# Splitting GpSimd's 128x512 additions and subtractions into two of 128x256

## The chip, the cores and the metric

The kernel runs on one core of one Trainium2 chip. The metric is the device time of one execution in microseconds (us), the median of three. TensorE is PE in the rows, its weight loads are PEld, VectorE is DVE, ScalarE is ACT, GpSimd is POOL, and SyncE with the DMA queue that it feeds is SP.

## The reference

64 sequences of 256 tokens with 256 features go through one decoder block. There are three attentions of 16 heads each, then a mixture of experts:

```
x = x + self_attention(layernorm(x))      # A: int8-quantized linears, causal softmax
x = x + cross_attention(layernorm(x))     # X: 120 context tokens, key mask, softmax with an extra zero
z = layernorm(x); y = z + self_attention(layernorm(z) * g1 + b1)   # F
x = x + y + moe(layernorm(y) * g2 + b2)   # F's end, then top-2 of 8 experts, 256 -> 1024 -> 256
```

All inputs and outputs are float32. Only the element-wise steps around queries, keys and residuals are touched by the change.

## The kernel before, in words

`attention(..., kind)` is called three times, for kinds A, X and F. Each call is one software-pipelined loop over the 64 sequences. In every turn of the loop each engine works through a fixed list of named steps (`SCHEDULE[kind][engine]`), written out by hand, and `LAG` and `SHIFTED` say for each name to which later or earlier sequence it belongs. So a turn holds parts of about nine sequences at once, and the order inside an engine never changes. The engines meet through semaphores only.

The steps that matter here, by their names in the lists:

- `maxima`: PE forms the scores of one head (L686 in F, L676 the last part in A, L681 in X) in one of three PSUM banks, and DVE reduces them to their maxima (L949). `attend`: PE forms the transposed scores (L658 in F), with ACT taking the exponential (L837). `pv0`, `pv1`: PE multiplies probabilities and values (L719 in F).
- `topA`, `topB`: DVE turns eight heads' maxima into two bfloat16 parts (L960 in A only, L962, L963), which PE transposes in `rowsA`, `rowsB` (L786).
- `q`, `k`: PE projects (L772), ACT evacuates and casts (L896, L911), then GpSimd subtracts the cast from the float32 value into `left` (L1119). `q_rest`, `k_rest`: ACT casts `left` to bfloat16 (L853), then GpSimd subtracts again and writes the third part (L1125). SP stores the three parts (L591), and loads them later in another layout (L536, L539).
- `xT`: PE transposes the normalized input, ACT evacuates it (L878 in F) for `q`.
- `fetch` in X: GpSimd adds a bias to the input (L1131), and DVE adds the projected attention of A to that (L990, step `wo`). `refetch`: GpSimd adds a bias to the residual read back (L1141 in X, L1146 in F), DVE adds the projection (L1083). `uapply` in F: DVE normalizes (`hn`, L1043), GpSimd forms `xu` (L1152) and then `h2 = hn * g` (L1156) and `h2 + b` (L1159), with a semaphore between these two.

GpSimd's and ACT's lists in F are, in order:

```
"POOL": ("k_rest q q_rest uapply refetch k")
"ACT": ("attend attend attend evac1 attend rowsB attend attend k_rest xT attend aT q attend attend q_rest "
        "attend attend rowsA attend evac0 h2T attend attend k attend attend")
```

GpSimd's `k` step and ACT's `k_rest` belong to the same sequence, with ACT's coming one turn list later. ACT goes on to `xT` only after `k_rest`, and PE's `q` waits for `xT`.

Of the kernel before, what the change touches and what calls it, by code (L numbers as in the profile page):

```python
# [5 lines left out]
ALU = mybir.AluOpType  # L6
# [21 lines left out]
def need(eng, sem, value):  # L28

    if isinstance(value, int) and value <= 0:  # L30
        return
    eng.wait_ge(sem, value)  # L32


def hold(eng, sem, value, passed):


    need(eng, sem, value)
    if not isinstance(value, int):
        eng.sem_inc(passed, 1)  # L40
# [306 lines left out]
def attention(nc, C, D, io, scratch, kind):  # L347
# [69 lines left out]
    def total(b, counts):  # L417

        if isinstance(b, int):
            return sum(turns(b, n) * c for n, c in counts)  # L420
        return b * sum(c for _, c in counts) + sum(LAG[n] * c for n, c in counts)

    def filling(g, name):

        b = g - LAG[name]
        if isinstance(b, int):
            n = total(b, [(u, 1) for u in UNITS]) + sum(present(b, u) for u in UNITS[:UNITS.index(name)])
            return n % 2, n // 2
        base = sum(LAG[u] for u in UNITS) + UNITS.index(name)
        return base % 2, NU // 2 * b + base // 2  # L430
# [12 lines left out]
    def iterations(eng):  # L443

        for b in range(FIRST, 3):
            yield b, b % 2
        with eng.Fori(0, (B - 8) // 2) as r:
            yield 2 * r + 3, 1
            yield 2 * r + 4, 0
        for b in range(B - 5, LAST + 1):  # L450
            yield b, b % 2

    def exists(g):

        return not isinstance(g, int) or 0 <= g < B

    def steps(b, par, engine):

        for name, i in STEPS[engine]:
            if present(b, name):  # L460
                yield name, i, b + LAG[name], (par + LAG[name]) % 2

    with ExitStack() as ctx:
# [13 lines left out]
        xin, grid = sb("xin", [P, 2, 256]), sb("grid", [P, 2, 256])  # L477
        xw, xT = sb("xw", [P, 2, 256], xdt), [sb(f"xT{i}", [P, 2, 256], xdt) for i in range(2)]
        q_f, k_f, left = sb("q_f", [P, 2, 256]), sb("k_f", [P, 2, 256]), {n: sb("left_" + n, [P, 2, 256]) for n in "qk"}
# [3 lines left out]
        aT, xres, zres = sb("aT", [P, 2, 256]), sb("xres", [P, 2, 256]), sb("zres", [P, 2, 256])  # L483
        based, summed = sb("based", [P, 2, 256]), sb("summed", [P, 2, 256])
# [12 lines left out]
        if kind == "X":  # L497
            yin, yint, yT = sb("yin", [P, 2, 256]), sb("yint", [P, 2, 256], BF16), sb("yT", [P, 2, 256], BF16)
            xb, x1, cin, ctxT = sb("xb", [P, 2, 256]), sb("x1", [P, 2, 256]), sb("cin", [120, 256]), [sb(f"ctxT{i}", [P, 2, 120]) for i in range(2)]
# [3 lines left out]
            y_in, y_ready, ctx_in, mask_in, mask_ready, maskT_ready, xb_ready, x1_out, xres_in, based_ready, mask_zero = (  # L503
                sem(n) for n in ("y_in", "y_ready", "ctx_in", "mask_in", "mask_ready", "maskT_ready", "xb_ready", "x1_out",
                                 "xres_in", "based_ready", "mask_zero"))
        if kind == "F":
            z, hn, h2, h2T = sb("z", [P, 2, 256]), sb("hn", [P, 2, 256]), sb("h2", [P, 2, 256]), sb("h2T", [P, 2, 256])
            xu = sb("xu", [P, 2, 256])
            ustats, umean_var, rstd_set = sb("ustats", [P, 2, 6]), sb("umean_var", [P, 2, 2]), sem("rstd_set")
            z_out, zres_in, xres_in, based_ready, hn_ready, xu_ready, h2_ready, h2_out = (  # L510
                sem(n) for n in ("z_out", "zres_in", "xres_in", "based_ready", "hn_ready", "xu_ready", "h2_ready", "h2_out"))

        with nc.Block() as block:
# [588 lines left out]
            @block.gpsimd  # L1102
            def _(pool):
                if kind == "X":
                    for m in mask:
                        nc.gpsimd.memset(m[:, :, :], 0.0).then_inc(mask_zero, 1)
                    pool.wait_ge(mask_zero, 2)
                for b, par in iterations(pool):
                    for name, i, g, gp in steps(b, par, "POOL"):
                        def drained(g, name):  # L1110
                            if exists(g):
                                bk, us = filling(g, name)
                                need(pool, work_drained[bk], us + 1)

                        if name in ("q", "k"):
                            src, parts, cast, rest, n = (q_f, q_parts, q_cast0, q_rest, 256) if name == "q" else \
                                (k_f, k_parts, k_cast0, k_rest, KT)
                            pool.wait_ge(cast, g + 1)
                            nc.gpsimd.tensor_tensor(left[name[0]][:, :, 0:n], src[:, :, 0:n], parts[:, 0, :, 0:n], ALU.subtract)\  # L1119
                                .then_inc(rest, 1)  # L1120
                        if name in ("q_rest", "k_rest"):
                            parts, cast, split, n = (q_parts, q_cast1, q_split, 256) if name[0] == "q" else \
                                (k_parts, k_cast1, k_split, KT)
                            pool.wait_ge(cast, g + 1)
                            nc.gpsimd.tensor_tensor(parts[:, 2, :, 0:n], left[name[0]][:, :, 0:n], parts[:, 1, :, 0:n], ALU.subtract)\  # L1125
                                .then_inc(split, 1)
                            pool.wait_ge(split, g + 1)
                        if name == "fetch" and kind == "X":
                            pool.wait_ge(x_in, 16 * g + 16)
                            drained(g - 1, "wo")  # L1130
                            nc.gpsimd.tensor_tensor(xb[:, :, :], xin[:, :, :], C["bo_a"][:, :, :], ALU.add).then_inc(xb_ready, 1)  # L1131
                        if name == "mload":
                            hold(pool, mask_in, 16 * g + 16, C["passed"])
                            hold(pool, score_full, G * (g - 1), C["passed"])
                            hold(pool, maskT_ready, g - 1, C["passed"])
                            nc.gpsimd.tensor_scalar(mask[gp][:, :, 0:120], mraw[:, :, :], MASKED, None, ALU.mult)\
                                .then_inc(mask_ready, 1)
                        if name == "refetch" and kind == "X":
                            pool.wait_ge(xres_in, 16 * g + 16)
                            drained(g - 1, "proj")  # L1140
                            nc.gpsimd.tensor_tensor(based[:, :, :], xres[:, :, :], C["bproj"][:, :, :], ALU.add)\  # L1141
                                .then_inc(based_ready, 1)
                        if name == "refetch" and kind == "F":
                            pool.wait_ge(zres_in, 16 * g + 16)
                            drained(g - 1, "proj")
                            nc.gpsimd.tensor_tensor(based[:, :, :], zres[:, :, :], C["bo_f"][:, :, :], ALU.add)\  # L1146
                                .then_inc(based_ready, 1)
                        if name == "uapply":
                            drained(g, "proj")
                            pool.wait_ge(xres_in, 16 * g + 16)  # L1150
                            need(pool, result_out, 16 * g)
                            nc.gpsimd.tensor_tensor(xu[:, :, :], summed[:, :, :], xres[:, :, :], ALU.add).then_inc(xu_ready, 1)  # L1152
                            pool.wait_ge(hn_ready, g + 1)
                            need(pool, h2_out, 16 * g)
                            drained(g - 1, "h2T")
                            nc.gpsimd.tensor_tensor(h2[:, :, :], hn[:, :, :], C["ln2_g"][:, :, :], ALU.mult)\  # L1156
                                .then_inc(h2_ready, 1)
                            pool.wait_ge(h2_ready, 2 * g + 1)
                            nc.gpsimd.tensor_tensor(h2[:, :, :], h2[:, :, :], C["ln2_b"][:, :, :], ALU.add)\  # L1159
                                .then_inc(h2_ready, 1)  # L1160
                            pool.wait_ge(h2_ready, 2 * g + 2)
                if kind == "A":
                    pool.wait_ge(link_v, total(LAST + 1, [(n, LINKS[n]) for n in ORDER]))
                    nc.gpsimd.partition_all_reduce(best_all[:, :], best[:, :], P, bass.bass_isa.ReduceOp.max)\
                        .then_inc(reduced, 1)
                    pool.wait_ge(reduced, 2)
# [811 lines left out]
```

## Time and profile before

| | |
|---|---|
| median of 3 executions | 5639.82 us (5639.09 to 5642.61) |
| profiled execution | 5645.5 us, with a span of 5643.8 us |
| busy of the span | PE 93%, DVE 81%, PEld 76%, ACT 64%, POOL 37% |
| loop A, X, F (about) | 120 to 1180 us, 1180 to 2370 us, 2370 to 3810 us |
| after the loops | routing and experts, in which the change touches nothing |

The span runs from the first to the last instruction of the profiled execution. The other 1.7 us of its time lie around it. Busy time of PE counts pipelined matmuls whose ends are modelled, so two of them can overlap, and a full PE row is not a PE at its peak. In a timeline row the first two numbers are the start and the length in microseconds, and several equal instructions are merged (x4). In square brackets stands the idle time before it, and who ended it.

### The profile page before, as it was taken

The numbers are of one execution on the slowest core, as the hardware profiler recorded it, in microseconds if no ns is written. First come the engines' busy times: TensorE is split into PE (matmuls) and PEld (weight loads), VectorE is DVE, ScalarE is ACT, GpSimd is POOL, SyncE is SP. The second block draws the span as 40 slices with busy tenths as digits, with TensorE's granted clock in tenths as the row PEclk, the third lists the DMA queues.
The fourth block names the chain that finished last, engine by engine and source line by source line (L and its number), as shares of the span: only waits on it lengthen the run. The fifth ranks groups of instructions, "written<-read, shape, count | busy, mean of one in ns | idle before, by whom it ended". The sixth has DMA issues, their size and how long they took to land. (4 is left out here: it accounts for less than half of the span.)

```text
span 5643.8 us, 154408 instructions
## 1 busy us (share of the span) xinstructions
PE 5221.8 (93%) x47388; PEld 4261.5 (76%) x47388; DVE 4582.0 (81%) x12204; ACT 3616.1 (64%) x7867; POOL 2071.9 (37%) x1753
## 2 busy tenths in 40 slices
PE   0899999979999999799999999996899999999998
PEld 0677777757777777667777777761799999899997
DVE  7788888868888888589999999979677777677776
ACT  4677777758888888667777777755344444444443
POOL 0322222213344334234444444430344444344443
PEclk9999999989999999999999999995899999999999
DMA  6777777746666666466666676742232322222221
GB/s 158 172 176 178 181 177 178 181 122 185 185 188 185 185 187 188 127 179 183 183 183 184 182 184 180 188 131 4 67 59 41 59 49 44 52 49 51 50 41 25
DMA packets 631734, 751.02 MB, mean 133 GB/s; under 512 B 143363, under 2 KB 560332, under 8 KB 631472
## 3 DMA queue, kind: packets, MB, share of 16 engines
q1 hardware_dynamic: 575136, 679.62, 46.1%
q0 software_dynamic: 49152, 63.10, 7.0%
q10 hardware_dynamic: 7184, 5.00, 0.5%
q8 instruction: 141, 2.31, 0.2%
q14 instruction: 121, 0.99, 0.1%
HBM read 476.49 MB, written 272.24 MB: 133 GB/s over the span
## 5 line engine op out<-in xcount | busy, mean ns | idle before, releaser
L837 ACT ACTIVATE F_probs<-F_scoreT 128x512 f32<-128x512 f32 x1024 | 587.5, 593 | 284.9 <-PE F_scoreT L658 276.4
L1862 POOL DMA_INDIRECT out_dram<-exp_gated,exp_token x256 | 424.6, 1658 | 886.7 <-DMA out_dram<-exp_gated,exp_token 330.7
L949 DVE TENSOR_REDUCE F_tops<-F_score 128x2 f32<-128x512 f32 x1024 | 671.3, 685 | 38.8 <-PE F_score L686 30.6
L949 DVE TENSOR_REDUCE A_tops<-A_score 128x3 f32<-128x384 f32 x1024 | 521.9, 553 | 69.2 <-PE A_score L676 49.5
L837 ACT ACTIVATE A_probs<-A_scoreT 128x384 f32<-128x384 f32 x1024 | 472.0, 486 | 91.2 <-PE A_scoreT L646 91.0
L949 DVE TENSOR_REDUCE X_tops<-X_score 128x4 f32<-128x484 f32 x512 | 325.7, 657 | 102.0 <-PE X_score L681 99.1
L686 PE MATMUL F_score<-KS,QS 96*128 96x256 bf16 x2048 | 381.2, 273 | 9.8 <-DVE F_tops L949 5.5
L658 PE MATMUL F_scoreT<-QS,KS 98*128 98x256 bf16 x2048 | 374.0, 274 | 1.5 <-ACT F_probs L837 1.2
L1843 POOL DMA_INDIRECT exp_x<-d_h,exp_token x256 | 283.5, 1107 | 179.5 <-DMA exp_b<-in_L_ffn_b_dram 101.8
L1639 ACT ACTIVATE exp_hT<-exp_hT,exp_b 128x512 f32<-128x512 f32 x512 | 338.7, 711 | 2.5 <-DVE exp_hT L1794 2.4
L671 PE MATMUL A_score<-causal,ident_b 128*128 128x256 bf16 x1024 | 283.0, 276 | 23.7 <-DVE A_tops L949 13.7
L837 ACT ACTIVATE X_probs<-X_scoreT 121x512 f32<-121x512 f32 x512 | 287.3, 587 | 26.6 <-PE X_scoreT L654 17.9
L642 PE MATMUL A_scoreT<-ident_b,causal 128*128 128x128 bf16 x2048 | 286.1, 221 | 3.0 <-ACT A_probs L837 1.5
L829 ACT ACTIVATE X_score<-X_mask 128x484 f32<-128x484 bf16 x512 | 283.5, 576 | 6.4 <-DVE X_tops L949 6.4
L674 PE MATMUL A_score<-KS,QS 96*128 96x256 bf16 x1024 | 281.5, 275 | 0.0
L646 PE MATMUL A_scoreT<-QS,KS 98*128 98x256 bf16 x1024 | 277.1, 271 | 0.0
L1673 ACT ACTIVATE exp_pair<-exp_lead 128x256 f32<-128x256 f32 x256 | 98.3, 384 | 262.1 <-PE exp_lead L1598 262.1
L658 PEld LDWEIGHTS F_scoreT<-QS,KS 98*128 98x128 bf16 x2048 | 175.4, 97 | 107.2 <-issue 53.1
L1664 ACT ACTIVATE exp_lone<-exp_lead 128x256 f32<-128x256 f32 x256 | 98.3, 384 | 244.1 <-PE exp_lead L1583 235.2
L1119 POOL TENSOR_TENSOR A_left_q<-A_q_f,A_q_parts 128x512 f32<-128x512 f32 x64 | 74.3, 1161 | 491.1 <-ACT A_q_parts L911 491.1
L719 PE MATMUL F_outs<-F_probs,V 128*32 128x256 f32 x4096 | 250.3, 385 | 0.7 <-ACT F_probs L837 0.7
L1559 PE MATMUL exp_side_r<-exp_w2s,exp_hTs 128*128 128x128 f32 x2048 | 249.6, 275 | 0.0
(397 smaller groups left out, 16141.3 us busy)
## 6 DMA issues: line engine op xcount, KB each, us to landing
QS<-d_q SPq DMA_DIRECT2D x384, 192.0 KB, 3.7
KS<-d_k SPq DMA_DIRECT2D x256, 192.0 KB, 4.2
QS<-d_q SPq DMA_DIRECT2D x384, 128.0 KB, 3.9
KS<-d_k SPq DMA_DIRECT2D x256, 128.0 KB, 4.0
d_q<-A_q_parts SPq DMA_DIRECT2D x64, 384.0 KB, 3.6
d_k<-A_k_parts SPq DMA_DIRECT2D x64, 384.0 KB, 2.7
QS<-d_q SPq DMA_DIRECT2D x384, 64.0 KB, 3.6
d_q<-X_q_parts SPq DMA_DIRECT2D x64, 384.0 KB, 2.9
```

Source lines behind the costliest of these rows:

```text
L642: mm(s[:, n * P:(n + 1) * P], C["causal"][:, 0:P], ident_b[:, :], start=n == 0, stop=False, skip_group_check=True)
L646: last = mm(s[:, P:384], k[0:98, i, 0:P], q[0:98, i, :], start=False, stop=True, skip_group_check=True)
L658: last = mm(s[:, n * 256:(n + 1) * 256], k[0:98, i, n * P:(n + 1) * P], q[0:98, i, :], start=True, stop=True)
L671: mm(s[:, 0:384].rearrange("p (n k) -> p n k", n=3)[:, 0:3:2, :], ident_b[:, :], C["causal"][:, :].rearrange("p (n k) -> p n k", n=2), sta ...
L674: mm(s[:, P:384], q[0:96, i, P:256], k[0:96, i, :], start=False, stop=False, skip_group_check=True)
L686: last = mm(s[:, n * 256:(n + 1) * 256], q[0:96, i, n * P:(n + 1) * P], k[0:96, i, :], start=True, stop=True)
L829: nc.scalar.activation(score[i % SB][:, 0:2 * HB * KN].rearrange("p (u n k) -> p u n k", u=HB, n=2), mask[gp][:, :, 0:KN].unsqueeze(1).bro ...
L837: nc.scalar.activation(probs[m][0:KR, at:at + HB, :].rearrange("p u x -> p (u x)"), scoreT[i % TB][0:KR, 0:HB * TCOL], ACT.Exp)\
L949: nc.vector.tensor_reduce(dst, src, AX.X, ALU.max).then_inc(score_read, 1)
L1639: nc.scalar.activation(hT[par][:, f, :], hT[par][:, f, :], ACT.Relu, bias=b1[k][:, f:f + 1])\
L1843: nc.gpsimd.indirect_dma_start(x[j % XB][:, s, :], None, scratch["h2"], bass.IndirectOffsetOnAxis(token[j % (2 * XB)][:, s:s + 1], 0), bou ...
L1862: nc.gpsimd.indirect_dma_start(out, bass.IndirectOffsetOnAxis(token[j % (2 * XB)][:, s:s + 1], 0), gated[par][:, s, :], None, bounds_check ...
```

## The change

Each `tensor_tensor` of GpSimd in the three loops is issued as two, one for each half of the middle index. Each half has 128x256 elements (128x120 for the keys in X). Only the second half raises the semaphore, so what waits for the result waits for both. Nothing waits between the halves. The multiplication at L1156 is split too. The mask step (L1136) is not. The diff, cut to its kinds (the same edit at every other place):

```diff
                             pool.wait_ge(cast, g + 1)
-                            nc.gpsimd.tensor_tensor(left[name[0]][:, :, 0:n], src[:, :, 0:n], parts[:, 0, :, 0:n], ALU.subtract)\
-                                .then_inc(rest, 1)
+                            for m in range(2):
+                                last = nc.gpsimd.tensor_tensor(left[name[0]][:, m, 0:n], src[:, m, 0:n], parts[:, 0, m, 0:n], ALU.subtract)
+                            last.then_inc(rest, 1)
...
-                            nc.gpsimd.tensor_tensor(parts[:, 2, :, 0:n], left[name[0]][:, :, 0:n], parts[:, 1, :, 0:n], ALU.subtract)\
-                                .then_inc(split, 1)
+                            for m in range(2):
+                                last = nc.gpsimd.tensor_tensor(parts[:, 2, m, 0:n], left[name[0]][:, m, 0:n], parts[:, 1, m, 0:n], ALU.subtract)
+                            last.then_inc(split, 1)
...
-                            nc.gpsimd.tensor_tensor(xb[:, :, :], xin[:, :, :], C["bo_a"][:, :, :], ALU.add).then_inc(xb_ready, 1)
+                            for j in range(2):
+                                last = nc.gpsimd.tensor_tensor(xb[:, j, :], xin[:, j, :], C["bo_a"][:, j, :], ALU.add)
+                            last.then_inc(xb_ready, 1)
...   (based in X and in F, xu: the same)
-                            nc.gpsimd.tensor_tensor(h2[:, :, :], hn[:, :, :], C["ln2_g"][:, :, :], ALU.mult)\
-                                .then_inc(h2_ready, 1)
+                            for j in range(2):
+                                last = nc.gpsimd.tensor_tensor(h2[:, j, :], hn[:, j, :], C["ln2_g"][:, j, :], ALU.mult)
+                            last.then_inc(h2_ready, 1)
                             pool.wait_ge(h2_ready, 2 * g + 1)
...   (h2 + ln2_b: the same)
```

## Rows read from the trace of the kernel before

**Rows 1.** Windows view, 1100 us of loop F: busy us by engine, clock, DMA.

```profile
core 0: us, PE busy (x) PEld busy (x) DVE busy (x) ACT busy (x) POOL busy (x), PEclk, DMA share, GB/s
2500.00:3600.00 1100.00, 1099.97 (x9691) 841.35 (x9690) 1014.05 (x2805) 793.19 (x1633) 493.44 (x408) 1.00 0.69 183
```

**Rows 2.** Groups by line and shape, GpSimd: busy us, mean ns, idle before.

```profile
L1119 POOL TENSOR_TENSOR F_left_k<-F_k_f,F_k_parts 128x512 f32<-128x512 f32 x64 | 74.2, 1159 | 2.0 <-ACT F_k_parts L911 2.0
...
L1119 POOL TENSOR_TENSOR X_left_k<-X_k_f,X_k_parts 128x240 f32<-128x240 f32 x64 | 40.1, 626 | 41.2 <-ACT X_k_parts L911 41.1
...
L1969 POOL MEMSET const-float32-1.0<- 128x1 f32 x1 | 0.1, 98 | 0.0
```

**Rows 3.** Waits, whole span: who waited for whom, total us, times, longest.

```profile
ACT F_k_parts L853 <- POOL F_left_k L1119: 28.8, 60, 1.3
...
DVE X_x L990 <- POOL X_xb L1131: 11.3, 9, 1.3
...
PEld X_work L802 <- DVE X_x L990: 8.7, 16, 1.5
```

**Rows 4.** Timeline of GpSimd, one turn of loop F.

```profile
3002.02 1.28 POOL L1156 TENSOR_TENSOR F_h<-F_hn,ln_g 128x512 f32<-128x512 f32 x1 [6.39 <-DVE logits L1088]
3003.38 1.27 POOL L1159 TENSOR_TENSOR F_h<-F_h,ln_b 128x512 f32<-128x512 f32 x1
3004.87 1.27 POOL L1146 TENSOR_TENSOR F_based<-F_zres,bo_f 128x512 f32<-128x512 f32 x1 [0.23 <-POOL F_h L1159]
3006.10 1.16 POOL L1119 TENSOR_TENSOR F_left_k<-F_k_f,F_k_parts 128x512 f32<-128x512 f32 x1
```

**Rows 5.** Timeline of ACT, the same turn.

```profile
3007.29 0.63 ACT L853 ACTIVATE F_k_parts<-F_left_k 128x512 bf16<-128x512 f32 x1 [0.45 <-POOL F_left_k L1119]
3007.83 1.00 ACT L878 ACTIVATE F_xT<-F_work,ln_b,ln_g 128x256 f32<-128x256 f32 x2
```

**Rows 6.** Timeline of PE and its weight loads, the same turn.

```profile
3008.31 0.77 PE L686 MATMUL F_score<-KS,QS 96*128 96x256 bf16 x4
...
3008.88 0.73 PEld L772 LDWEIGHTS F_work<-F_xT,w_fq 128*128 128x128 f32 x4
```

**Rows 7.** Timeline of DVE, the same turn to the start of the next.

```profile
3002.06 1.27 DVE L963 TENSOR_TENSOR F_top_parts<-F_tops,F_top_parts 128x16 bf16<-128x16 f32 x1
...
3004.68 1.28 DVE L949 TENSOR_REDUCE F_tops<-F_score 128x2 f32<-128x512 f32 x2
3006.10 0.26 DVE L1067 RECIPROCAL F_rec<-F_work 128x16 f32<-128x16 f32 x1
...
3016.65 0.69 DVE L949 TENSOR_REDUCE F_tops<-F_score 128x2 f32<-128x512 f32 x1 [0.38 <-PE F_score L686]
...
3022.69 0.41 DVE L1043 TENSOR_SCALAR F_hn<-F_summed,F_umean_var,F_rstd 128x256 f32<-128x256 f32 x1
```

**Rows 8.** Groups by line and shape, DVE: small operations of the three loops.

```profile
L963 DVE TENSOR_TENSOR F_top_parts<-F_tops,F_top_parts 128x16 bf16<-128x16 f32 x128 | 91.3, 713 | 4.4
...
L960 DVE TENSOR_TENSOR A_tops<-A_tops 128x8 f32<-128x8 f32 x128 | 50.8, 397 | 12.6 <-DVE A_tops L949 0.3
...
L962 DVE CAST X_top_parts<-X_tops 128x16 bf16<-128x16 f32 x128 | 44.0, 344 | 0.1
...
L963 DVE TENSOR_TENSOR A_top_parts<-A_tops,A_top_parts 128x16 bf16<-128x16 f32 x128 | 23.8, 186 | 4.4
```

**Rows 9.** Timeline of DVE in loop A, after `topB`.

```profile
711.91 0.56 DVE L949 TENSOR_REDUCE A_tops<-A_score 128x3 f32<-128x384 f32 x1 [0.62 <-PE A_score L676]
```

**Rows 10.** Timeline of GpSimd and DVE in loop X.

```profile
2037.58 1.27 POOL L1131 TENSOR_TENSOR X_xb<-X_xin,bo_a 128x512 f32<-128x512 f32 x1
2037.80 1.09 DVE L962 CAST X_top_parts<-X_tops 128x16 bf16<-128x16 f32 x1
2038.81 1.16 POOL L1119 TENSOR_TENSOR X_left_q<-X_q_f,X_q_parts 128x512 f32<-128x512 f32 x1
2038.92 1.07 DVE L963 TENSOR_TENSOR X_top_parts<-X_tops,X_top_parts 128x16 bf16<-128x16 f32 x1
```

More of the change, by code:

```diff
@@ L1140, in _ @@
                             drained(g - 1, "proj")
-                            nc.gpsimd.tensor_tensor(based[:, :, :], xres[:, :, :], C["bproj"][:, :, :], ALU.add)\
-                                .then_inc(based_ready, 1)
+                            for j in range(2):
+                                last = nc.gpsimd.tensor_tensor(based[:, j, :], xres[:, j, :], C["bproj"][:, j, :], ALU.add)
+                            last.then_inc(based_ready, 1)
                         if name == "refetch" and kind == "F":
@@ L1145, in _ @@
                             drained(g - 1, "proj")
-                            nc.gpsimd.tensor_tensor(based[:, :, :], zres[:, :, :], C["bo_f"][:, :, :], ALU.add)\
-                                .then_inc(based_ready, 1)
+                            for j in range(2):
+                                last = nc.gpsimd.tensor_tensor(based[:, j, :], zres[:, j, :], C["bo_f"][:, j, :], ALU.add)
+                            last.then_inc(based_ready, 1)
                         if name == "uapply":
@@ L1151, in _ @@
                             need(pool, result_out, 16 * g)
-                            nc.gpsimd.tensor_tensor(xu[:, :, :], summed[:, :, :], xres[:, :, :], ALU.add).then_inc(xu_ready, 1)
+                            for j in range(2):
+                                last = nc.gpsimd.tensor_tensor(xu[:, j, :], summed[:, j, :], xres[:, j, :], ALU.add)
+                            last.then_inc(xu_ready, 1)
                             pool.wait_ge(hn_ready, g + 1)
@@ L1155, in _ @@
                             drained(g - 1, "h2T")
-                            nc.gpsimd.tensor_tensor(h2[:, :, :], hn[:, :, :], C["ln2_g"][:, :, :], ALU.mult)\
-                                .then_inc(h2_ready, 1)
+                            for j in range(2):
+                                last = nc.gpsimd.tensor_tensor(h2[:, j, :], hn[:, j, :], C["ln2_g"][:, j, :], ALU.mult)
+                            last.then_inc(h2_ready, 1)
                             pool.wait_ge(h2_ready, 2 * g + 1)
-                            nc.gpsimd.tensor_tensor(h2[:, :, :], h2[:, :, :], C["ln2_b"][:, :, :], ALU.add)\
-                                .then_inc(h2_ready, 1)
+                            for j in range(2):
+                                last = nc.gpsimd.tensor_tensor(h2[:, j, :], h2[:, j, :], C["ln2_b"][:, j, :], ALU.add)
+                            last.then_inc(h2_ready, 1)
                             pool.wait_ge(h2_ready, 2 * g + 2)
```

## The prediction, made before the changed kernel was built or timed

> **What bounds the kernel now.** I read the busy shares first, then the windows of each loop, the waits, the groups by shape, and last the timeline of one turn of loop F. GpSimd is busy for only 37% of the span, so its own length is no bound. What matters is whether someone waits for a GpSimd result, or is held up while GpSimd works. In loop F the PE row is full: 1099.97 of 1100 us, with DVE behind it at 1014 and GpSimd at 493 [rows 1]. The turns of F are nearly identical, so one turn can be read for all. The waits name one place in F where another engine stands still for GpSimd: ACT's `k_rest` cast waits for `left_k` 60 times, for 28.8 us in all [rows 3]. The timeline shows why. At the end of a turn DVE finishes `hn`, and then GpSimd runs four operations in a row: `h2` product, `h2` sum, `based`, `left_k`, from 3002.02 to 3007.26 [rows 4]. The only pauses are those of its semaphores, and the fourth starts 0.04 us before the third ends. ACT's cast starts at 3007.29, 0.03 after `left_k`, having idled 0.45, and the two `xT` evacuations follow and end at 3008.83 [rows 5]. PE runs four score matmuls from 3008.31, and its first weight load of the `q` projection comes at 3008.88 [rows 6]. So PE reaches `q` when `xT` has been ready for 0.05 us: the chain over GpSimd is as long as PE's own way to this point.
>
> The ring closes. Behind `q` PE works on to the scores for which DVE idles 0.38 at 3016.65, and from there DVE has no idle time worth naming until the next `hn` at 3022.69 [rows 7]. This `hn` starts the next four operations of GpSimd. Anything that lengthens the four is added to every turn, once the 0.05 us are used up.
>
> **The change, part by part.** The cost of a split is the fixed part of one more instruction. For subtractions two widths are there: 1159 ns for 512 columns and 626 for 240 [rows 2]. That is 533/272 = 1.96 ns a column and 156 ns fixed. Two halves in a row are 2 x (156 + 502) = 1316 ns, less the 0.04 us by which a GpSimd instruction without a wait overlaps the one before it [rows 4]: about 1.27 us, or 0.11 more than now. Additions and the product take 1.27 to 1.28 us [rows 4]. I scale the fixed part with the length (1275/1159), to 0.17, less 0.04: 0.13 more each. These additions are not seen at another width, so the cost is bounded. Below by the shortest instruction, 98 ns for one column [rows 2]: 0.06 each. Above by assuming that the halves don't overlap but part by 0.09, as the product and the sum do, with a semaphore between them (3.38 less 3.30) [rows 4]: 0.26 each. I take the middle value, since it comes from the same operation.
>
> The Trainium skill speaks to this in "GPSIMD Engine Reference", section 3.1: it gives 4497 ns for a float32 add of 2048 columns. With the 1.28 us here for 512, that makes an estimate of 0.20 us fixed and 0.16 more for each split add, and the sum below would be about 5670. No run here shows that width.
>
> Loop F: three splits at 0.13 and one at 0.11 in the chain are 0.50. Less the 0.05 of slack, that is 0.45 a turn. The wait shows up in 60 turns [rows 3]: 60 x 0.45 = +27 us. With the bounds: 4 x 0.06 - 0.05 = 0.19, or +11 us, and 4 x 0.26 - 0.05 = 0.99, or +59 us. The other GpSimd steps of F (`q`, `q_rest`, `k_rest`, `xu`) end long before their readers need them: GpSimd idles 6.39 us ahead of the product [rows 4]. ACT's `q_rest` may start 0.1 later, in a part of the turn in which it waits for PE soon after, so I cost it at nothing. If that cover were gone it would be 6 us more. SP issues the store of the key parts when L1125 has ended, and its loads are for a turn later, so they move with the turn.
>
> Loop A: GpSimd's results have readers that come microseconds later, and no wait for GpSimd of any size is on the list. I put the four splits of a turn, 4 x 0.11 us, at nothing.
>
> Loop X: `xb` gets 0.13 longer, and DVE's L990 waits for it 9 times, 11.3 us. PE then waits for L990 16 times, 8.7 us [rows 3]. The next part works the other way there.
>
> **What DVE gets back.** DVE's small operations stretch while GpSimd works. L963, the same 128x16 operation, takes 186 ns on average in A but 713 in F. L960 takes 397 and X's cast 344 [rows 8]. In F it started at 3002.06, just after the product, and ended at 3003.33, with the product's end at 3003.30 [rows 4, 7]. It stood still until GpSimd's instruction was over. Over the loops that is (713-186) x 128 = 67 us in F, (397-186) x 128 = 27 in A and (344-186) x 128 = 20 in X for these three groups. A shorter GpSimd instruction frees DVE sooner: at about 3002.74 in F, 0.6 us earlier. Does it slip in between two halves that follow without a pause? In X it did between two such instructions: the cast ended at 2038.89, when `xb` ended at 2038.85 and `left_q` had been issued at 2038.81. The next L963 then stood still until 2039.99, through `left_q` [rows 10]. So each GpSimd boundary lets one DVE operation through, and GpSimd lost nothing by it (1.16 as ever).
>
> The gain in F comes to nothing as I read it. After L963 come two reductions and more, and then `tok0`, for which DVE has already idled: 3005.96 to 3006.10 [rows 7]. What DVE reaches sooner it waits for, since PE's order sets it. In A DVE idles 0.62 us for PE right after the stretched operation [rows 9]. In X some of PE's 8.7 us for L990 can come back, as the cast and L963 ahead of it stand still for shorter pieces, less the 0.13 of `xb`. I take 2 us, between 0 and 8.7.
>
> The Trainium skill describes the same thing in "SBUF — State Buffer", section "Who interferes with whom": a DVE instruction with two SBUF inputs and a GpSimd one that reads SBUF hold a shared port for the whole instruction, and the second one blocks. The trace agrees (1.27 us for a 0.18 us operation). By that rule alone the change is a gain for DVE. It is the first rival.
>
> **The sum.** Own time of the profiled execution: 5643.8 span and 1.7 around it, 5645.5. Plus 27 in F, less 2 in X: 5670.5. The median shown is 5.7 lower, so on the runs' scale it is 5639.8 + 25 = **5665 us**, +0.44%.
>
> **The rivals.**
> 1. Faster: DVE is the bound and gets back about half of the 67 + 27 + 20 us, 57 us. With the +27 of the chain that gives 5640 + 27 - 57 = 5610. For it: DVE is busy for 1014 of 1100 us and stretched in every turn. Against it: the idle time behind each stretched operation (0.14 in F, 0.62 in A). It decides if the 0.14 us in F is not a wait for PE but a fixed pause of DVE, for then the 0.6 us reaches PE. Chance 0.09.
> 2. No change to speak of: the fixed part is at its lower bound, or the chain has more room than the 0.05 I read, for instance because the `q` weight load waits for something else. +11 in F less 2 in X: 5649, and down to 5640 if the slack is 0.2 us a turn. Chance 0.17.
> 3. More than forecast: the halves don't overlap. +59 - 2: 5697. Against it: instructions without a wait between them overlap by 0.04 now. The place is the same chain. Chance 0.12.
> 4. GpSimd keeps DVE out through both halves. Then each stretched DVE operation ends 0.13 later than now. F's 0.14 of idle time just covers that, X loses the 2 us gained and about 2 more, and the total is 5640 + 27 + 2 = 5669, which cannot be told from the forecast by time alone. Against it is what the cast did in X. It is counted with the forecast.
>
> **How the numbers follow.** Forecast with rival 4: chance 0.62, about 5653 to 5680. A measurement of this kernel can tell about 0.2%, 11 us. Faster by more: rival 1, 0.09, plus 0.01. Within 0.2%: rival 2, 0.17, plus 0.01 of the forecast's low edge. Slower: 0.61 of the forecast and rival 3's 0.12 less a little, 0.72. The range leaves out rival 1 and the upper part of rival 3, and takes in rival 2: 5642 to 5688.
>
> **What would show it.** A half should take 0.66 us (subtraction) to 0.72 (addition), with starts 0.62 to 0.68 apart. From the start of the product to the end of `left_k` it should be 5.74 us instead of 5.24. ACT's wait for `left_k` should go from 0.45 to about 0.9 a turn, and a wait of PE's weight load L772 for `xT` should appear, near 0.4 a turn. The time from one product to the next should grow by 0.45 us. L963's mean in F should fall from 713 to about 450 ns, and DVE's wait at `tok0` should grow by 0.5. The turn of A should keep its length. Wrong would be the forecast if PE's `q` starts as early after `hn` as now, or if a half costs more or less than 0.11 to 0.13 beyond its share.

## The result, and the profile after

The changed kernel takes 5682.36 us (median of 4 runs, 5676.52 to 5688.64), beside 5639.45 us for the kernel before in the same comparison: the ratio is 1.0076, with a 95% interval of 1.0059 to 1.0094. The forecast was 5665 us, slower by 25 us, with a range of 5642 to 5688. It is slower by 43 us. The direction and the place were right, and the size was too small. Of all the executions behind this document one, of e3_ax below, ran at a much lower granted clock (9357.73 us at 0.698, where the others have 0.971 to 0.976), and it is left out of the medians and ratios.

The first thing to read is where in the program the time went. Each loop begins with a MEMSET of DVE at L917, so the starts of those, and of the two stages behind the loops, cut the profiled execution into parts:

| us | A | X | F | routing | experts |
|---|---|---|---|---|---|
| before | 1081.3 | 1157.9 | 1445.0 | 141.7 | 1685.2 |
| after | 1079.0 | 1153.3 | 1490.3 | 141.7 | 1683.7 |

Loop F is 45.3 us longer, and nothing else is longer. The differences add up to 36.9 us, and with 0.4 less ahead of loop A that is the 36.5 us between the spans of the two profiled executions (5643.8 and 5680.3). The medians are 43 us apart, because the profiled execution of the kernel before was itself 6 us above its median. The same 1100 us of loop F as in [rows 1], in the windows view of the changed kernel (its columns are those of [rows 1]):

```profile
2500.00:3600.00 1100.00, 1069.77 (x9339) 810.76 (x9337) 979.40 (x2703) 770.75 (x1574) 532.51 (x790) 1.00 0.67 177
```

PE's row was full and no longer is: PE stands idle for 30 of 1100 us. PE also does fewer instructions in that time, 9339 instead of 9691, because the turns are longer. The granted clock is 1.00 in both, so the clock has no part in it. GpSimd's own busy time rose, but it is still under half of the window.

The halves themselves, in the groups by line and shape (busy us, mean ns):

```profile
L1166 POOL TENSOR_TENSOR F_h<-F_hn,ln_g 128x256 f32<-128x256 f32 x128 | 90.9, 730 | 390.5 <-DVE logits L1088 364.1 <-DVE F_hn L1043 26.4
...
L1153 POOL TENSOR_TENSOR F_based<-F_zres,bo_f 128x256 f32<-128x256 f32 x128 | 90.4, 727 | 19.9 <-POOL F_h L1170 12.8 <-DMA F_zres<-d_z 6.6
...
L1120 POOL TENSOR_TENSOR F_left_k<-F_k_f,F_k_parts 128x256 f32<-128x256 f32 x128 | 83.1, 670 | 1.5 <-ACT F_k_parts L911 1.5
...
L963 DVE TENSOR_TENSOR F_top_parts<-F_tops,F_top_parts 128x16 bf16<-128x16 f32 x128 | 56.3, 440 | 4.4
...
L1120 POOL TENSOR_TENSOR X_left_k<-X_k_f,X_k_parts 128x120 f32<-128x120 f32 x128 | 49.2, 405 | 25.9 <-ACT X_k_parts L911 25.6
```

A half of an addition takes 0.73 us, a half of a subtraction 0.67. GpSimd's timeline has one turn of loop F; a row with x2 holds both halves, from the start of the first to the end of the second:

```profile
3001.69 1.30 POOL L1120 TENSOR_TENSOR F_left_q<-F_q_f,F_q_parts 128x256 f32<-128x256 f32 x2 [3.29 <-ACT F_q_parts L911]
3003.73 1.31 POOL L1127 TENSOR_TENSOR F_q_parts<-F_left_q,F_q_parts 128x256 bf16<-128x256 f32 x2 [0.74 <-ACT F_q_parts L853]
3005.31 1.41 POOL L1160 TENSOR_TENSOR F_xu<-F_summed,F_xres 128x256 f32<-128x256 f32 x2 [0.27 <-POOL F_q_parts L1127]
3012.91 1.42 POOL L1166 TENSOR_TENSOR F_h<-F_hn,ln_g 128x256 f32<-128x256 f32 x2 [6.20 <-DVE logits L1088]
3014.41 1.41 POOL L1170 TENSOR_TENSOR F_h<-F_h,ln_b 128x256 f32<-128x256 f32 x2
3016.04 1.42 POOL L1153 TENSOR_TENSOR F_based<-F_zres,bo_f 128x256 f32<-128x256 f32 x2 [0.23 <-POOL F_h L1170]
3017.43 1.29 POOL L1120 TENSOR_TENSOR F_left_k<-F_k_f,F_k_parts 128x256 f32<-128x256 f32 x2
```

Two halves of 0.73 take 1.42 together, so the second starts 0.04 us before the first ends, as forecast. A split costs 1.30 - 1.16 = 0.14 us for a subtraction and 1.41 - 1.27 = 0.14 for an addition. From the start of the product to the end of `left_k` it is 3018.72 - 3012.91 = 5.81 us, and it was 5.24 [rows 4].

Who waits for it, in the timelines of ACT, PE and its weight loads in the same turn (compare [rows 5] and [rows 6]):

```profile
3018.74 0.63 ACT L853 ACTIVATE F_k_parts<-F_left_k 128x512 bf16<-128x512 f32 x1 [1.22 <-POOL F_left_k L1120]
3019.28 1.00 ACT L878 ACTIVATE F_xT<-F_work,ln_b,ln_g 128x256 f32<-128x256 f32 x2
```

```profile
3018.99 0.77 PE L686 MATMUL F_score<-KS,QS 96*128 96x256 bf16 x4
3020.34 1.99 PE L772 MATMUL F_work<-F_xT,w_fq 128*128 128x256 f32 x8 [0.58 <-ACT F_xT L878]
```

```profile
3020.34 1.59 PEld L772 LDWEIGHTS F_work<-F_xT,w_fq 128*128 128x128 f32 x8 [0.86 <-ACT F_xT L878]
```

This is the forecast chain, row by row: `left_k` ends at 3018.72, the cast starts 0.02 later, `xT` is ready at 3020.28, and PE, which had finished its four score matmuls, stood idle until then. Before, the weight load came 3008.88 - 3002.02 = 6.86 us after the product's start [rows 4, 6]; now it is 3020.34 - 3012.91 = 7.43, later by 0.57.

The waits over the whole span (us in total, times, longest) say that this happens in every turn, against [rows 3]:

```profile
ACT F_k_parts L853 <- POOL F_left_k L1120: 76.5, 61, 1.5
...
PEld F_work L772 <- ACT F_xT L878: 53.5, 60, 1.5
...
PE F_work L772 <- ACT F_xT L878: 41.2, 59, 4.8
...
DVE X_x L990 <- POOL X_xb L1135: 24.1, 19, 1.4
...
PEld X_work L802 <- DVE X_x L990: 3.5, 11, 0.7
```

The size is what does not fit. The chain became 0.57 us longer, but ACT's wait went from 0.45 to 1.22 us, and the wait of the weight load from nothing to 0.86. To see how much longer a turn is, I use an operation that DVE does once a turn: L106, the first step of the square root for `F_rstd`. The view of that one line gives count, durations and first and last start (ns: shortest, median, longest). Before:

```profile
L106 DVE TENSOR_SCALAR F_rstd<-F_rstd x51: 160/161/164, 2521.0 to 3599.6; 128x6 int32<-128x6 int32 x51
```

and after:

```profile
L106 DVE TENSOR_SCALAR F_rstd<-F_rstd x49: 357/372/443, 2513.8 to 3588.2; 128x6 int32<-128x6 int32 x49
```

A turn took (3599.6 - 2521.0)/50 = 21.57 us and takes (3588.2 - 2513.8)/48 = 22.38. That is 0.81 more, where 0.45 was forecast. And the row shows something that no step of the forecast held: L106 itself, with the same 128x6 elements, takes 372 ns instead of 161. DVE's timeline shows what it ran into:

```profile
3004.50 0.56 DVE L1017 TENSOR_SCALAR F_rstd<-F_umean_var 128x2 f32<-128x2 f32 x1
3004.98 1.48 DVE L949 TENSOR_REDUCE F_tops<-F_score 128x2 f32<-128x512 f32 x2
3006.37 0.37 DVE L106 TENSOR_SCALAR F_rstd<-F_rstd 128x6 int32<-128x6 int32 x1
...
3012.95 0.72 DVE L963 TENSOR_TENSOR F_top_parts<-F_tops,F_top_parts 128x16 bf16<-128x16 f32 x1
3013.82 0.69 DVE L949 TENSOR_REDUCE F_tops<-F_score 128x2 f32<-128x512 f32 x1
3014.56 0.69 DVE L1057 SCALAR_TENSOR_TENSOR V<-F_work,bvF 128x512 f32<-128x512 f32 x1
...
3016.78 0.26 DVE L1067 RECIPROCAL F_rec<-F_work 128x16 f32<-128x16 f32 x1 [0.33 <-PE F_work L791]
```

L106 ends at 3006.74, and GpSimd's `xu` ended at 3005.31 + 1.41 = 3006.72. L106 stood still as L963 did, behind another GpSimd operation. In the kernel before it did not, but only just: `xu` ended at 3015.99 + 1.27 = 3017.26, and L106 started at 3017.26. GpSimd and DVE of the kernel before, each in its timeline:

```profile
3015.99 1.27 POOL L1152 TENSOR_TENSOR F_xu<-F_summed,F_xres 128x512 f32<-128x512 f32 x1 [0.34 <-POOL F_q_parts L1125]
...
3015.39 0.29 DVE L1017 TENSOR_SCALAR F_rstd<-F_umean_var 128x2 f32<-128x2 f32 x1
...
3017.26 0.16 DVE L106 TENSOR_SCALAR F_rstd<-F_rstd 128x6 int32<-128x6 int32 x1
```

So the new theory has two parts. **The chain**: four splits between `hn` and PE's `q` weight load. **The side**: the splits of `left_q`, `q_parts` and `xu`, which make `xu` end later and hold L106, behind which DVE has no idle time to give before the next `hn`: averaged over the turns from 2600 to 3550 us, `hn` starts 5.27 to 5.28 us after L106 ends, in each of the twelve kernels. Together by the medians 0.57 + (0.372 - 0.161) = 0.78 of the 0.81. L106 lasts about 0.36 us in some turns and 0.44 in others, so its mean, 404 ns, is what adds up over the turns: 0.57 + (0.404 - 0.161) = 0.81. The eighth split of F, that of `k_parts`, is in neither part, and nothing is left for it.

### The profile page after: what moved, and what is told of

Its sections match the earlier page's. It is cut to its first block and busy times, and to the rows that moved or that the text cites. A ratio compares the mean times of both kernels' runs of the same rounds, so it can differ in the third digit from the quotient of the medians.

```text
span 5680.3 us, 155559 instructions
## 1 busy us (share of the span) xinstructions
PE 5224.1 (92%) x47387; PEld 4254.0 (75%) x47388; DVE 4574.2 (81%) x12204; ACT 3625.3 (64%) x7867; POOL 2233.5 (39%) x2905
## 5 line engine op out<-in xcount | busy, mean ns | idle before, releaser
L949 DVE TENSOR_REDUCE F_tops<-F_score 128x2 f32<-128x512 f32 x1024 | 671.3, 684 | 25.7 <-PE F_score L686 10.9
L949 DVE TENSOR_REDUCE A_tops<-A_score 128x3 f32<-128x384 f32 x1024 | 520.5, 553 | 67.1 <-PE A_score L676 48.3
L949 DVE TENSOR_REDUCE X_tops<-X_score 128x4 f32<-128x484 f32 x512 | 325.7, 657 | 96.2 <-PE X_score L681 93.9
L1120 POOL TENSOR_TENSOR A_left_q<-A_q_f,A_q_parts 128x256 f32<-128x256 f32 x128 | 83.3, 671 | 473.9 <-ACT A_q_parts L911 473.9
```

The source lines that it names most:

```text
L949: nc.vector.tensor_reduce(dst, src, AX.X, ALU.max).then_inc(score_read, 1)
```

## The experiments

All ten kernels come from one source, in which each of GpSimd's additions, subtractions and the product goes through a helper that splits it or not by a list:

```diff
+SPLIT = [...]
...
+                def part(key, out, a, b, op):
+                    if kind + key not in SPLIT:
+                        return nc.gpsimd.tensor_tensor(out, a, b, op)
+                    for m in range(2):
+                        last = nc.gpsimd.tensor_tensor(out[:, m, :], a[:, m, :], b[:, m, :], op)
+                    return last
```

Lines of the loops' other code are 2 higher in their profiles than before (L949 is L951, L772 is L774), and all GpSimd's operations carry the helper's line, L1108 where whole and L1110 where split. Each was timed against the kernel before on the same chip. The turn is worked out from the row of L106 of each kernel, as above; "L106" is its median and its mean in the same window.

| kernel | us | before | ratio, 95% interval | loop F | turn | L106, ns |
|---|---|---|---|---|---|---|
| before | | | | 1445.0 | 21.57 | 161, 161 |
| after | 5682.36 | 5639.45 | 1.0076, 1.0059 to 1.0094 | 1490.3 | 22.38 | 372, 404 |
| e1_chain | 5677.45 | 5641.18 | 1.0066, 1.0053 to 1.0079 | 1476.8 | 22.15 | 161, 162 |
| e2_side | 5655.42 | 5641.18 | 1.0029, 1.0018 to 1.0039 | 1457.2 | 21.81 | 396, 398 |
| e3_ax | 5638.42 | 5641.18 | 0.9998, 0.9989 to 1.0007 | 1443.1 | 21.57 | 161, 161 |
| e4_all_swap | 5632.39 | 5641.18 | 0.9987, 0.9978 to 0.9996 | 1440.2 | 21.50 | 361, 393 |
| e5_swap | 5642.19 | 5643.31 | 0.9996, 0.9987 to 1.0005 | 1440.4 | 21.50 | 161, 161 |
| e6_swap_chain | 5640.29 | 5643.31 | 0.9996, 0.9987 to 1.0005 | 1441.1 | 21.50 | 160, 160 |
| e7_xu | 5644.02 | 5643.31 | 1.0000, 0.9991 to 1.0009 | 1444.0 | 21.58 | 163, 168 |
| e8_q | 5651.56 | 5643.31 | 1.0019, 1.0010 to 1.0028 | 1448.4 | 21.66 | 284, 253 |
| e9_swap_side | 5642.20 | 5644.06 | 0.9999, 0.9989 to 1.0008 | 1438.8 | 21.52 | 398, 397 |
| e10_swap_side_mult | 5641.81 | 5644.06 | 0.9993, 0.9984 to 1.0002 | 1439.7 | 21.50 | 400, 400 |

e3_ax has loop F as it was. Its 1443.1 beside 1445.0 us shows that the length of loop F is known to about 2 us only, while the turn, 21.57 in both, is known to 0.01.

### The chain alone

```diff
+SPLIT = ['Fmult', 'Fadd', 'Fbased', 'Fleft_k']
```

> Only the four operations of F's chain are split: product, sum, based, left_k. Theory (the ring over GpSimd's four operations and ACT's k_rest): the chain takes 5.81 us in place of 5.24, PE reaches q about 0.53 us later in each of 60 turns, +32 us, about 5671. Nothing else of F gets longer: the DVE operation L106 stays at 0.16 us. Rival (all 45 us of F sit in the chain): +45 us, 5685. Rival (DVE's earlier release in F pays): less than +20 us.

Loop F is 31.8 us longer than before. The row of L106:

```profile
L106 DVE TENSOR_SCALAR F_rstd<-F_rstd x50: 160/161/164, 2501.9 to 3587.0; 128x6 int32<-128x6 int32 x50
```

(3587.0 - 2501.9)/49 = 22.145, or 0.57 us more a turn, which is what the four splits add to the chain, to the hundredth. L106 is not stretched. The waits of the window from 2500 to 3600 us show ACT and PE at the place of the forecast, 1.03 and 0.66 us a turn:

```profile
ACT F_k_parts L855 <- POOL F_left_k L1110: 51.4, 50, 1.3
...
PEld F_work L774 <- ACT F_xT L880: 32.4, 49, 0.9
```

### The side alone

```diff
+SPLIT = ['Fleft_q', 'Fq_parts', 'Fxu']
```

> Only left_q, q_parts and xu of F are split, none of the chain. Theory (xu now ends after DVE has reached L106, which stands still for it, in a stretch in which DVE has no idle time before hn): L106 takes 0.37 us or more in place of 0.16, and the turn is 0.2 to 0.3 us longer, +12 to +18 us, 5652 to 5658. Rival (as the prediction had it, these ends are covered): 0 us.

```profile
L106 DVE TENSOR_SCALAR F_rstd<-F_rstd x50: 359/396/441, 2515.8 to 3584.7; 128x6 int32<-128x6 int32 x50
```

The turn is (3584.7 - 2515.8)/49 = 21.81, 0.24 more, and L106 is 396 - 161 = 235 ns longer. Loop F grew by 12.2 us. The two parts add up: 31.8 + 12.2 = 44.0 of the 45.3 us, and by the turns 0.57 + 0.24 = 0.81. The whole times, 36 and 14 us above the kernel before where the change has 43, allow the same within their intervals. GpSimd and DVE, each in its timeline, show the meeting; `xu` ends at 3018.06, L106 at 3018.09:

```profile
3016.65 1.41 POOL L1110 TENSOR_TENSOR F_xu<-F_summed,F_xres 128x256 f32<-128x256 f32 x2 [0.34 <-POOL F_q_parts L1110]
...
3017.66 0.43 DVE L106 TENSOR_SCALAR F_rstd<-F_rstd 128x6 int32<-128x6 int32 x1
```

### The side in two doses

```diff
# e7_xu
+SPLIT = ['Fxu']
# e8_q
+SPLIT = ['Fleft_q', 'Fq_parts']
```

> Only xu of F is split. Theory (L106 ends 0.02 to 0.04 us after the GpSimd operation that it meets, and costs only what lies beyond its own 0.16): xu ends at 16.24 us of the turn, L106 would have ended at 16.30, so nothing: 0 to 1 us in loop F. Rival (any lengthening of xu is paid): 0.13 a turn, +8 us.

> Only left_q and q_parts of F are split, so xu stays whole but starts about 0.26 us later. Theory: xu ends at 16.37 us of the turn, L106 at 16.39 in place of 16.30, 0.09 a turn, +4 to +7 us in loop F. Rival (what costs is ACT's or SP's later q_rest and store, not L106): L106 stays at 0.16 us and the turn grows all the same.

If the meeting of `xu` and L106 is the cause, the cost is not proportional to the splits. L106 lasts 0.16 us anyway, and only what `xu` reaches past that can cost. In the averages over the turns from 2600 to 3550 us, L106 of the kernel before starts 0.03 us after `xu` ends and so ends 0.19 after it, and a held L106 ends 0.03 after it: that leaves 0.16. Counted from the start of `left_q`, `xu` ends 0.14 us later in e7_xu than before, 0.26 in e8_q and 0.40 in e2_side, so the cost should be 0, 0.10 and 0.24. The rows of L106, first of e7_xu, then of e8_q:

```profile
L106 DVE TENSOR_SCALAR F_rstd<-F_rstd x51: 159/163/179, 2518.8 to 3598.0; 128x6 int32<-128x6 int32 x51
```

```profile
L106 DVE TENSOR_SCALAR F_rstd<-F_rstd x51: 210/284/297, 2504.1 to 3587.3; 128x6 int32<-128x6 int32 x51
```

One split costs nothing (turn 21.58, time ratio 1.0000). Two cost 0.09 us a turn, and three cost 0.24. The means of L106, 253 and 398 ns, are above 161 by just that; the median of e8_q, 284, is not, as its turns fall into two kinds. A cost of 0, 0.09, 0.24 for one, two and three splits rules out that each split has a price of its own.

There is a second small operation that could be blamed. L1017, two reductions ahead of L106, meets `q_parts` in the same way: it takes 0.30 us before, and 0.55 to 0.56 in e8_q, e2_side and the changed kernel. But before the second of the two reductions DVE waited 0.38 us for PE's scores [rows 7], and this wait fell to 0.11 or 0.12 in the three. L1017's delay is covered by it. The doses say the same: L1017 is equally long in e8_q and e2_side, and the turns are 0.15 us apart, as the means of L106 are.

The time of e8_q went up by 8 us (5.6 to 15.8 by the interval), the turns by 64 x 0.09 = 6, loop F in the profiled execution by 3.4; these agree only as far as such small numbers can.

### Loops A and X alone

```diff
+SPLIT = ['Aleft_k', 'Ak_parts', 'Aleft_q', 'Aq_parts', 'Xleft_k', 'Xk_parts',
+         'Xleft_q', 'Xq_parts', 'Xxb', 'Xbased']
```

> Only the operations of loops A and X are split, F is as before. Theory: A keeps its length, X gains 3 to 7 us by DVE's shorter stand-stills ahead of L990, about 5634. Rival (the 7 us by which A and X were shorter are chance of that execution): 0 us, 5640.

Nothing that can be measured: the 5634 us that I expected is missed. A is 1081.5 us long and X 1158.7, beside 1081.3 and 1157.9. The changed kernel's X was 4.6 us shorter. But X lies between 1155.6 and 1164.3 us in the nine kernels of this study that have it as it was, and it took 1153.3, 1158.6 and 1158.7 in the three that have it split. Those means, 1160.4 and 1156.9, are no further apart than one kernel's X is from another's, so a gain of a few us in X is neither shown nor excluded; by the interval of the whole time, 6 us is its upper end.

### The chain with left_k taken out of it

Another way to test the chain is to keep every split and shorten the chain instead. In loop F's order for GpSimd, `k` moves ahead of `refetch`, so that `left_k` no longer waits behind `based`:

```diff
-        "POOL": ("k_rest q q_rest uapply refetch k"),
+        "POOL": ("k_rest q q_rest uapply k refetch"),
```

e4_all_swap has this with all the splits of the change, e5_swap has it with none, and e6_swap_chain with those of e1_chain.

> All splits of the change, and in F's list of GpSimd k goes before refetch, so based is no longer ahead of left_k. Theory: the chain to left_k is shorter than before the change, ACT no longer waits for it and PE no longer for xT. What is left is L106's stand-still, +12 to +18 us, less 3 to 7 in X: 5645 to 5655. Rival (the chain isn't what costs): as the changed kernel, 5680.

> Nothing is split, only k goes before refetch in F's list of GpSimd. Theory (PE itself reached q only 0.05 us before xT was ready, and DVE is still held up 1.1 us by the whole product): loop F loses at most that slack, 0 to 5 us, 5636 to 5641. Rival (the order is worth more than the splits cost): -10 us or more.

> Product, sum, based and left_k of F are split and k goes before refetch; left_q, q_parts and xu stay whole, and so do A and X. Theory (with the chain off the ring, what is left is DVE's earlier release from the product, worth about 0.3 us a turn, and no stand-still of L106): L106 at 0.16 us, the turn at 21.2 to 21.35 us, 13 to 22 us less than before, about 5622. Rival (the release of DVE is worth nothing in F, as the prediction had it): as the swap alone, 5636 to 5641.

Here are the rows of L106 of e4_all_swap, e5_swap and e6_swap_chain:

```profile
L106 DVE TENSOR_SCALAR F_rstd<-F_rstd x51: 353/361/439, 2517.3 to 3592.3; 128x6 int32<-128x6 int32 x51
```

```profile
L106 DVE TENSOR_SCALAR F_rstd<-F_rstd x52: 160/161/163, 2501.2 to 3597.7; 128x6 int32<-128x6 int32 x52
```

```profile
L106 DVE TENSOR_SCALAR F_rstd<-F_rstd x52: 159/160/161, 2500.1 to 3596.6; 128x6 int32<-128x6 int32 x52
```

(3592.3 - 2517.3)/50, (3597.7 - 2501.2)/51 and (3596.6 - 2500.1)/51 are all 21.50. One line of order takes away the whole 45 us of loop F and some 3 to 5 us more. Since the swap alone shortens the turn, the chain of the kernel before was already 0.07 us longer than what bounds the turn without it. PE's busy row could not tell this: it reads 1099.97 of 1100 us before and 1100.00 with the swap. e4_all_swap, at 0.9987, is below the kernel before and the changed one; e5_swap has the same turn, and the two cannot be told apart by their intervals. So the splits are no gain, and the 0.07 us a turn is that of the order.

My expectation for e4_all_swap, 5645 to 5655, was a miss: L106 is still held there (mean 393 ns), and costs nothing. Why is shown below. That for e6_swap_chain, 5622 us, was a miss too. I had thought that with `left_k` out of the way the earlier release of L963 would pass on to PE. ACT's timeline of e6_swap_chain shows why it can't:

```profile
3005.64 0.62 ACT L855 ACTIVATE F_k_parts<-F_left_k 128x512 bf16<-128x512 f32 x1
3006.62 1.02 ACT L880 ACTIVATE F_xT<-F_work,ln_b,ln_g 128x256 f32<-128x256 f32 x2 [0.36 <-PE F_work L761]
```

`xT` waits 0.36 us for PE's own transposes, and no longer for GpSimd. PE goes through its order without a stop at `q`, and DVE's 0.55 us is time in which DVE waits. I read 21.50, which four kernels with the swap share, as the length of PE's list.

### The side, with the chain out of the way

```diff
# e9_swap_side: the swap, and
+SPLIT = ['Fleft_q', 'Fq_parts', 'Fxu']
# e10_swap_side_mult: the swap, and
+SPLIT = ['Fleft_q', 'Fq_parts', 'Fxu', 'Fmult']
```

> k before refetch, and only left_q, q_parts and xu split; the product stays whole. Theory (L106's 0.24 us comes late on DVE, and with the whole product DVE has only 0.13 us of idle time at tok0 to swallow it): the turn is 21.50 + 0.11 = about 21.61 us, loop F some 7 us longer than with the swap alone, about 5648. Rival (with the chain off the ring, nothing on DVE matters up to 0.24 us, as in the run with all splits and the swap): 21.50 us.

> As the one before, and the product split as well. Theory (DVE's L963 is now released 0.55 us sooner, which covers the 0.24 us of L106): the turn is back at 21.50 us, about 5641. Rival (the release of DVE is worth nothing anywhere): the same turn as the one before it.

```profile
L106 DVE TENSOR_SCALAR F_rstd<-F_rstd x52: 359/398/440, 2501.2 to 3599.0; 128x6 int32<-128x6 int32 x52
```

```profile
L106 DVE TENSOR_SCALAR F_rstd<-F_rstd x52: 364/400/442, 2500.6 to 3597.1; 128x6 int32<-128x6 int32 x52
```

In e9_swap_side L106 is stretched by 237 ns, as in e2_side, but a turn is (3599.0 - 2501.2)/51 = 21.525 us: 0.025 over the floor, where e2_side paid 0.24. The same delay of DVE has a price only while the chain is the bound: then `hn` being late is added to the next turn. With the swap, `hn` can be 0.2 us later against PE's order before PE notices. The expected 21.61 was too high; it allowed DVE too little room. In e10_swap_side_mult the product's split lets L963 go 0.55 us earlier, and DVE waits for PE again, 16.5/51 = 0.32 us a turn, in the waits of the same window:

```profile
DVE F_rec L1069 <- PE F_work L793: 16.5, 51, 0.3
```

e9_swap_side has no such wait. So the release of L963 is real room for DVE, and in e10 it buys the 0.025 us that was left to buy.

## Why the prediction was right in direction and too small

**What bounds the kernel: right.** The chain `hn`, product, sum, `based`, `left_k`, `k_rest`, `xT`, `q` sets the turn of loop F. e1_chain lengthens it by 0.57 and the turn grows by 0.57, and the swap takes it out and the turn falls to 21.50.

**The price of a split: mis-sized.** "I scale the fixed part with the length (1275/1159), to 0.17, less 0.04: 0.13 more each", and 0.11 for the subtraction. Measured is 0.14 for both. The 156 ns fixed came from 512 against 240 columns, and 512 against 256 give 2 x 670 - 1159 = 181. Over the four splits this is 0.57 in place of 0.50. The bounds, 0.06 and 0.26, held it. The upper bound has a slip: the pause between product and sum is 3.38 - 3.30 = 0.08 and not 0.09, which makes it 0.25. The estimate from the Trainium skill, "GPSIMD Engine Reference", section 3.1, was 0.16: 0.02 too much, where mine were 0.01 and 0.03 too little.

**The slack of 0.05 us: there was none.** The prediction took it from a weight load that came 0.05 us after `xT` was ready. But in e1_chain the turn grows by the full 0.57, and e5_swap shows that the chain before was 0.07 us too long already, with nothing to spare. Averaged over the turns from 2600 to 3550 us, it is 16.14 us from the start of `hn` to L106 before and 16.70 after. PE's first `q` matmul comes 7.79 us after `hn` starts before and 8.32 after, only 0.53 later, and the other 0.04 lie behind it: from that matmul to the reduction ahead of L106 it is 7.73 us before and 7.77 after. The slack is worth 3 us in all.

**"The other GpSimd steps of F ... end long before their readers need them ... so I cost it at nothing": this is the step that failed.** The sentence is true of the readers. Nobody who reads `q_parts` or `xu` waits longer. The one who pays is L106, which reads neither of them and only wants to run while `xu` does. I had the mechanism in hand, for L963, and used it for gains alone. The section of the Trainium skill that I named, "SBUF — State Buffer", "Who interferes with whom", also lists `tensor_scalar` among the operations that can take the shared port pair, and `tensor_reduce` as one that never does. The trace agrees with both: L106 and L1017 are held, and L949 takes 0.69 us beside GpSimd's product (3013.82), though it reads its scores from PSUM and so tests the second little. I read it for the two-input operations only; I never asked which DVE operations the longer GpSimd steps would newly meet. The row that would have told me lay in the timeline: `xu` ends at 3017.26 and L106 starts at 3017.26. It is worth 12.2 us in e2_side. "If that cover were gone it would be 6 us more" priced ACT's delay of 0.1 us a turn, and no meeting with DVE; what counts is the sum of the three splits ahead of `xu`'s end, 0.40, less L106's own 0.16, or 0.24 a turn.

**What DVE gets back: right, to the step.** L963 fell from 713 to 440 ns (forecast about 450). It ended at 3013.67 in the turn shown; the first half of the product, 0.73 us from 3012.91, ended at 3013.64, and the second was not late. So DVE slips in between halves, and rival 4 is out. DVE's idle time at `tok0` rose by 0.20 and not by 0.5: before, `tok0` came 4.97 us after `hn`'s start, and now it comes at 3016.78 - 3012.02 = 4.76, and of the two pieces of work between (L949 at 3013.82, 0.69 long, and L1057 at 3014.56) the second now starts 0.05 us after the first ends, where such neighbours overlap by 0.09 when DVE doesn't wait. 0.20 + 0.21 + 0.14 = 0.55, so all of the release became waiting or lateness of `hn`, and none of it came to PE. "The gain in F comes to nothing" holds; e6_swap_chain shows it without the chain.

**Loops A and X.** A at nothing is right (e3_ax). The 2 us gained in X stay open: PE's wait for L990 fell from 8.7 to 3.5 us, as the step said, while DVE's for `xb` rose from 11.3 to 24.1, and what is left of it is smaller than X's own spread.

**The sum.** Forecast 27 - 2 = +25. Measured in loop F 45.3: 0.57 x 60 turns = 34 by the chain (31.8 in e1_chain, which is 0.57 x 56; the last five turns of the loop are shorter and did not grow), 12 by the side. Of the 18 us by which the loop outgrew the forecast 27, 12 are the side, which the sum had at nothing, and 5 are the chain (31.8 - 27): price of a split and slack, with fewer turns against them. The rest is within the 2 us to which the length of the loop is known.

**The rivals.** Rival 1 (DVE is the bound, faster) fell: half the stretch was given back and no time with it. Rival 2 (little change) fell: a split costs 0.14 us and not 0.06, and with 0.2 us of slack e1_chain's turn would have grown by 0.37, where it grew by 0.57. Rival 3 came as near in time (5697) as the forecast (5665), for another reason than its own: the halves overlap by 0.04. Rival 4 fell as said.

**The checks.** Halves 0.67 and 0.73 (0.66, 0.72); product to end of `left_k` 5.81 (5.74); ACT's wait 1.22 (0.9) and the weight load's 0.86 (0.4), both larger because the turn grew by 0.81 and not 0.45, and their own work did not; turn +0.81 (+0.45).

## What to carry to other kernels

When a GpSimd operation gets longer or moves, look not only for who reads its result but for which small DVE operations run at its end: a DVE operation that starts just as GpSimd ends has no margin but its own length (0.16 us for L106), and what it is late by is added to the turn if DVE has no idle time to give behind it and the loop's ring runs through it. L1017 had such idle time behind it, and cost nothing. The price of such a meeting begins at a threshold, so parts of a change that cost nothing each can cost something together, and they should be tried together and in doses. Where several operations of one engine stand in a ring, look at their order as well as at their sizes: here `k_rest` waited for `left_k` alone, and with `left_k` ahead of `based` the splits of the chain cost nothing.

## What the runs showed of the hardware that was not expected

- A very small DVE operation is held until a GpSimd instruction ends as well: 128x6 int32 (L106, 161 ns before, 372 in the median after) and 128x2 float32 (L1017, 0.56 us in the turn shown, held until `q_parts` ended at 3005.04). When held, both end 0.02 to 0.03 us after the GpSimd instruction that they met.
- A held DVE operation goes in at the boundary of two GpSimd instructions that follow each other with 0.04 us of overlap, and the pair is no longer for it (1.42 us with L963 between, 1.41 to 1.42 without).
- GpSimd's float32 subtraction takes 405 ns for 120 columns, 670 for 256 and 1159 for 512 (two rows of 256); an addition takes 730 and 1275 ns. One instruction more costs about 0.18 us, less the overlap.
